# Quantised rows turned by transposing transfers instead of by TensorE, and the work between the attention loops dealt anew

## The reference, cut to what matters

```python
def block(x, ctx):
    x = x + attention(layernorm(x), ctx, ctx)        # 16 heads of 32, causal mask, Wq Wk Wv Wo with biases
    return x + ffn(layernorm(x))

def bit_linear(x, w):                                # act_quant: per row, 127 / max|x|, rounded; w: ternary
    return act_quant(x) @ weight_quant(w).T

def ffn(x):
    h = bit_linear(x, w1)                            # 512 -> 2048
    h = depthwise_conv1d(h, conv_w, conv_b)          # three taps along the rows
    return bit_linear(silu(h), w2)                   # 2048 -> 512
```

## Time and profile before

| what | value |
|---|---|
| time, median of 3 runs | 1520.56 us (1520.53 to 1521.53) |
| time of the profiled execution | 1520.43 us |
| its span, first to last instruction | 1518.6 us |
| mean granted clock of TensorE | 0.988 |
| PE busy | 1460.6 us, 96% of the span |
| DVE busy | 1278.0 us, 84% |
| ACT busy | 1185.3 us, 78% |
| POOL busy | 1028.7 us, 68% |

### The profile page before, as it was taken

How to read it: one execution, slowest core, us unless ns; L and a number is a source line. 1 busy time by engine, 2 the same in 40 slices (tenths; PEclk the granted TensorE clock), 3 DMA queues, 4 the chain that set the end, 5 groups by cost and what they waited for, 6 DMA issues and landing times. The chain is left out here.

```text
span 1518.6 us, 24856 instructions
## 1 busy us (share of the span) xinstructions
PE 1460.6 (96%) x9102; PEld 892.5 (59%) x9102; DVE 1278.0 (84%) x2002; ACT 1185.3 (78%) x2190; POOL 1028.7 (68%) x834
## 2 busy tenths in 40 slices
PE   9998988999999999999999999999999999999898
PEld 6474655657575665657575665657575655656343
DVE  5787796898979889898979898897979898887877
ACT  3567788979787888979687888979687888978763
POOL 4011567868675977968675977968675877968543
PEclk8999899999999999999999999999999999999999
DMA  8561002021310303030310303030210202020001
GB/s 258 148 193 42 29 8 71 8 80 32 76 43 12 94 8 99 8 93 19 75 44 18 88 8 99 8 100 14 73 43 23 84 8 71 8 71 1 31 1 56
DMA packets 80343, 85.21 MB, mean 56 GB/s; under 512 B 29983, under 2 KB 55839, under 8 KB 79709
## 3 DMA queue, kind: packets, MB, share of 16 engines
q1 hardware_dynamic: 80221, 83.62, 19.1%
HBM read 38.74 MB, written 19.42 MB: 38 GB/s over the span
## 5 line engine op out<-in xcount | busy, mean ns | idle before, releaser
L675 POOL TENSOR_TENSOR h<-h,gall 128x512 f32<-128x512 f32 x233 | 343.9, 1476 | 18.3
L660 POOL TENSOR_TENSOR h<-h,r 128x512 f32<-128x512 f32 x240 | 307.0, 1322 | 52.5 <-ACT r L1222 50.6
L673 POOL TENSOR_TENSOR gall<-gall,cw 128x512 f32<-128x512 f32 x233 | 255.3, 1096 | 112.6 <-DVE h L1751 112.6
L1751 DVE SCALAR_TENSOR_TENSOR h<-gall,cw,h 128x512 f32<-128x512 f32 x249 | 253.2, 1020 | 47.6 <-ACT h L1320 47.4
L885 PEld LDWEIGHTS ps<-va,pexp 128*128 128x128 f32 x2048 | 259.5, 192 | 29.0 <-issue 10.9
L1676 DVE SCALAR_TENSOR_TENSOR gall<-ps,bias,srow 128x512 f32<-128x512 f32 x256 | 191.1, 747 | 94.3 <-POOL h L675 57.9
L891 PE MATMUL ps<-xqT,w1T 128*128 128x512 f16 x1024 | 255.1, 379 | 6.6 <-DVE gall L1676 6.5
L885 PE MATMUL ps<-va,pexp 128*128 128x33 f32 x2048 | 257.7, 270 | 0.0
L1085 PE MATMUL ps<-w2T,hqb 128*128 128x512 fp8e4 x960 | 242.4, 380 | 0.0
L1320 ACT ACTIVATE h<-gall,cb,cw 128x512 f32<-128x512 f32 x249 | 216.3, 869 | 8.3
L1301 ACT ACTIVATE pexp<-ps 128x512 f32<-128x512 f32 x320 | 179.8, 589 | 54.5 <-PE ps L854 27.9
(11 more groups left out here) (226 smaller groups left out, 2336.8 us busy)
## 6 DMA issues: line engine op xcount, KB each, us to landing
qs<-hl SPq DMA_DIRECT2D x192, 128.0 KB, 2.4
xr<-in_x SPq DMA_DIRECT2D x16, 1024.0 KB, 5.4
out<-xr SPq DMA_DIRECT2D x64, 256.0 KB
h<-in_L_ffn_w SPq DMA_DIRECT2D x8, 1024.0 KB, 5.4
srow<-in_L_xattn_bo SPq DMA_DIRECT2D x15, 256.0 KB, 3.3
kst<-kh_scratch SPq DMA_DIRECT2D x32, 38.5 KB
xr<-in_ctx SPq DMA_DIRECT2D x1, 1024.0 KB
h<-in_L_xattn_Wk SPq DMA_DIRECT2D x1, 1024.0 KB, 8.2
```

Of the source, the lines that this page charges most:

```text
L660: gp.tensor_tensor(hc(c), hc(c), r2[:], ALU.mult).then_inc(u_ok, 1)
L673: gp.tensor_tensor(right, right, cw[:, c, 2:3].to_broadcast([P, TB]), ALU.mult).then_inc(c2m_ok, 1)
L675: gp.tensor_tensor(hc(c), hc(c), right, ALU.add).then_inc(c2p_ok, 1)
L1751: ve.scalar_tensor_tensor(out=hc(c), in0=g[:, c % 4, 1:TB + 1], scalar=cw[:, c, 1:2], in1=hc(c), op0=ALU.mult, op1=ALU.add).then_inc(c1_ok, 1)
```

## The change

1. turn_xq, its 16 transposes and its four PSUM copies are gone. As each of the four quantised row tiles is ready, SP issues a transposing transfer from it (hlq, now with adjacent elements) straight into xqT. mm1_ahead(0) waits for these.
2. The hidden absmax has three pieces: column tiles 0 to 3 in the attention loop ahead of the last tap, 4 to 11 after at_low, 12 to 15 after residual(0); two merges in place of one.
3. q_low moves ahead: two of them after residual(1), two after residual(2). Nothing lies between norm2 and quantise any more.
4. ACT squares tiles 0 and 1 before it centres tiles 2 and 3.
5. In the late_results slots PE runs mm2(0), the first two query_scores, spread_scales, half of mm2(1), and then steps n = 2 to 15: four matmuls of mm2 in each of n = 2 to 7, two in each from n = 8 on. result(1) comes after the fourth maximum.

```diff
         def hlq(i):
-            return osb[:, i, :].bitcast(F16)[:, 0:2 * D:2]
+            return osb[:, i, :].bitcast(F16)[:, 0:D]
@@ SP
+                if do_a:
+                    for i in range(TT):
+                        sp.wait_ge(xq_ok, at(s, TT, i + 1))
+                        sp.dma_start(xqT[:, :, i * P:(i + 1) * P], hlq(i), transpose=True).then_inc(xq_turned, 16)
                 if do_m and do_a:
                     store_rows(range(2 if late_results(s) else TT))
@@ PE
-                        pe.wait_ge(xqc, at(s, KT, KT))
+                        pe.wait_ge(xq_turned, at(s, 16 * TT, 16 * TT))
...
                 def turn_pm():
-                    pe.wait_ge(pm_ok, at(s, 3, 2 if s == NB else 0))
+                    pe.wait_ge(pm_ok, at(s, 5, 0))
...
+                elif late_results(s):
+                    mm2(0)
+                    query_scores(0, 0)
+                    query_scores(0, 1)
                 elif do_a and do_m:
                     mm2(0)
                     mm2(1)
...
-                if do_a and do_m and s != NB - 1:
-                    mm2(2, range(0, 8))
+                if late_results(s):
+                    mm2(1, range(0, 8))
                 if s == NB - 1:
                     mm2(2)
                     mm2(3, range(0, 11))
-                    turn_xq(range(KT))
...
                 for n in range(0 if s == NB - 1 else TT * NG):
-                    if do_q:
+                    if do_q and not (late_results(s) and n < 2):
                         query_scores(n // NG, n % NG)
...
-                    if do_a and do_m:
-                        if n < 4:
-                            mm2(2, range(8 + 2 * n, 10 + 2 * n))
-                        elif n < 13:
-                            mm2(3, MM2_LAST[n - 4])
+                    if late_results(s):
+                        if n in (2, 3):
+                            mm2(1, range(4 * n, 4 * n + 4))
+                        elif 4 <= n < 8:
+                            mm2(2, range(4 * n - 16, 4 * n - 12))
+                        elif 8 <= n < 15:
+                            mm2(3, range(2 * n - 16, 2 * n - 14))
+                        elif n == 15:
+                            mm2(3, range(14, 15))
+                            mm2(3, range(15, 16))
...
-                    if do_a and n in (13, 14):
-                        turn_xq((n - 13,))
-                    if do_a and n == 15:
-                        turn_xq((2, 3))
@@ ACT
                     centre(1)
...
+                    square(0)
+                    square(1)
+                    if late_results(s):
+                        offset(1)
                     centre(2)
...
                     centre(3)
-                    if late_results(s):
-                        offset(1)
-                    for i in range(TT):
-                        square(i)
+                    square(2)
+                    square(3)
...
-                    if do_a:
-                        act.wait_ge(xqt_ok, at(s, KT, k + 2 - k % 2))
-                        copy(xqT[:, k, :], xq_half(s, k)).then_inc(xqc, 1)
@@ DVE
+                def absmax(a, b, o):
                     dve.wait_ge(si_ok, at(s, CT, 2 * b - CT))
+                    if a == 6 and do_a:
+                        dve.wait_ge(pm_ok, at(s, 5, 3 - 5))
                     ve.tensor_reduce(o[:], h[:, a:b].rearrange("p a t e -> p t a e"), AX.XY, ALU.max,
                                      apply_absolute_value=True).then_inc(pm_ok, 1)
...
+                    if do_f and do_a and c == CT + 1:
+                        absmax(0, 2, pm)
                     if do_f and c >= 2 and not on_pe(s, c - 2):
                         taps(c - 2)
...
                 if do_f and do_a:
-                    absmax(0)
-                    if s == NB - 1:
-                        residual(0)
-                    absmax(1)
-                    if s == NB - 1:
-                        residual(1)
-                    merge()
+                    absmax(2, 6, r2)
+                    merge(r2, 2)
+                    residual(0)
+                    absmax(6, 8, r2)
+                    merge(r2, 4)
+                    residual(1)
...
-                    if s < NB - 1:
+                    if s == 0:
                         residual(0)
                         residual(1)
+                    if s > 0 and do_q:
+                        q_low(0)
+                        q_low(1)
+                    centred_max(0)
                     residual(2)
-                    centred_max(0)
+                    if s > 0 and do_q:
+                        q_low(2)
+                        q_low(3)
+                    centred_max(1)
                     residual(3)
-                    centred_max(1)
...
-                if s > 0 and do_q:
-                    q_low(0)
-                    q_low(1)
...
                 if do_a:
                     norm2()
-                if s > 0 and do_q:
-                    q_low(2)
-                    q_low(3)
...
                     result(0)
-                    result(1)
+                    if not late_results(s):
+                        result(1)
...
                     if do_q:
                         maximum(n // NG, n % NG)
+                    if late_results(s) and n == 3:
+                        result(1)
```

More of the change, by code:

```diff
@@ L321, in build @@
         dgs_ok = sem("dgs_ok")
-        xqt_ok = sem("xqt_ok")
-        xqc = sem("xqc")
+        xq_turned = sem("xq_turned")
         sr_ok = sem("sr_ok")
@@ L419, in score_tiles @@
             return range(NS * c // n, NS * (c + 1) // n) if c < n else range(0)
-        MM2_LAST = [range(2 * n, 2 * n + 2) for n in range(7)] + [range(14, 15), range(15, 16)]
         LATE = (TT - 1) * P
@@ L582, in slot @@
                         sp.wait_ge(q, 16 * NB)
-                    sp.wait_ge(xqt_ok, KT * NB)
+                    sp.wait_ge(xq_turned, 16 * TT * NB)
                     for bb in range(NBATCH):
@@ L922, in mm1_ahead @@
                         pe.wait_ge(src, at(s, 1, 1))
+                    if c == 1 and do_q:
+                        pe.wait_ge(mtc, at(s, 2, 3))
                     mm1(c)
@@ L1033, in turn_maxima @@
                     r.then_inc(mt_ok, 1)
-                def turn_xq(ks):
-                    for k in ks:
-                        if k == 0:
-                            pe.wait_ge(xq_ok, at(s, TT, TT))
-                        if k == 2 and do_q:
-                            pe.wait_ge(mtc, at(s, 2, 3))
-                        bank = xq_half(s, k)
-                        for i in range(TT):
-                            r = tp(bank[:, i * P:(i + 1) * P], hlq(i)[:, k * P:(k + 1) * P], identh[:])
-                        r.then_inc(xqt_ok, 1)
                 def spread_row():
@@ L1756, in taps, with merge @@
                                                 in1=hc(c), op0=ALU.mult, op1=ALU.add).then_inc(c2_ok, 1)
-                def absmax(k):
-                    dve.wait_ge(si_ok, at(s, CT, 8 * (k + 1) - CT))
-                    ve.tensor_reduce((pm, r2)[k][:], h[:, 4 * k:4 * k + 4].rearrange("p a t e -> p t a e"), AX.XY, ALU.max,
-                                     apply_absolute_value=True).then_inc(pm_ok, 1)
-                def merge():
-                    dve.wait_ge(pm_ok, at(s, 3, 2 - 3))
-                    ve.tensor_tensor(pm[:], pm[:], r2[:], ALU.max).then_inc(pm_ok, 1)
-                def absmax_last(a, b, o):
+                def absmax(a, b, o):
                     dve.wait_ge(si_ok, at(s, CT, 2 * b - CT))
+                    if a == 6 and do_a:
+                        dve.wait_ge(pm_ok, at(s, 5, 3 - 5))
                     ve.tensor_reduce(o[:], h[:, a:b].rearrange("p a t e -> p t a e"), AX.XY, ALU.max,
                                      apply_absolute_value=True).then_inc(pm_ok, 1)
-                def merge_last(o, n):
-                    dve.wait_ge(pm_ok, at(s, 3, n - 3))
+                def merge(o, n):
+                    dve.wait_ge(pm_ok, at(s, 5, n - 5))
                     ve.tensor_tensor(pm[:], pm[:], o[:], ALU.max).then_inc(pm_ok, 1)
@@ L1806, in attention @@
                     elif k == 0:
-                        dve.wait_ge(xqt_ok, at(s, KT, 0))
+                        dve.wait_ge(xq_turned, at(s, 16 * TT, 0))
                     dve.wait_ge(rz_ok, at(s, NG, k + 1))
@@ L1909, in slot @@
                     if s == NB and c == 16:
-                        absmax_last(0, 4, pm)
+                        absmax(0, 4, pm)
                         fix_absmax()
@@ L1935, in slot @@
                 if s == NB:
-                    absmax_last(4, 6, r2)
-                    merge_last(r2, 2)
+                    absmax(4, 6, r2)
+                    merge(r2, 2)
                     fix_scales()
-                    absmax_last(6, 8, pexp[:, 0, :])
-                    merge_last(pexp[:, 0, :], 4)
+                    absmax(6, 8, pexp[:, 0, :])
```

(1 more changed line is left out.)

3 lines of the change are left out of this document (removed).

## The result

The changed kernel takes 1556.38 us (median of 4 runs, 1554.38 to 1559.19) against 1520.55 us (4 runs) of the kernel before: a ratio of 1.0245, 95% interval 1.0226 to 1.0263. The profiled execution has a span of 1554.9 us and a mean granted clock of 0.978 (before 1518.6 and 0.988). It is slower, by the amount and for the reason forecast; three terms of the sum were off by 1 to 3 us each, partly against each other. One of all the runs reported here was a slow one (1539.56 us, of e6_both_even), and its ratio leaves it out.

A forecast was written before the change was run, and what follows sets the result against it. The prediction took PE and DVE, side by side between the loops, as the bound, with PE stalling on DVE. 1520.4 + 24.7 (slots) + 8.5 (clock) + 1.3 (edges) = 1555 us; 8-in-10 range 1521 to 1582.

The forecast's parts named there:

- DVE's chain: DVE's steps from the tap to the maxima in slot 6: first maximum at 663.2 against 663.79, 0.6 us sooner.
- The slots: PE stalls 1.2 us at turn_pm and 2.4 at the third query: +1.9 us per slot, 24.7 in 13.
- The clock: Granted clock halves behind the new PE stall in five of 13 slots, 1.7 us each: +8.5 us, bounds 0 and 22.
- The edges: Slot 0 about -1, slot 1 +1, slot 15 +2, masked slots 3, 7, 11 together -0.7: sum +1.3 us.
- the transfers' term of 0: Transposing transfers land before mm1_ahead(0) needs them, so cost 0; they would count from 3.4 us each in series.
- The total: Whole kernel: 1555 us, 2.3% slower; 8-in-10 range 1521 to 1582, the forecast's own range 1536 to 1578.
- the third rival: Transfers are late: at 5 us each in series, 6.2 behind the need in 15 slots, +93, about 1650 us; chance 0.12.
- the sum of 21 us: Estimate by the skill's table for transposing 16 blocks by DMA in series: 21 us, 7 us too late in every slot.
- negmT in the queue: In SP's queue the maxima stand behind the transfers and two result rows, but are ready at 677 only.
- the first: Rival: PE isn't held and the transposes are simply gone, stretch 20.55 in place of 22.10, 1500 us; chance 0.07.
- The second: Rival: DVE sets the end as before, PE's stalls stay inside its slack, 1522 us, up to 1535; chance 0.11.

The follow-up runs named there:

- e6_both_even: The changed kernel with residual(2) and two q_low right behind residual(1), two q_low behind norm2, first queries later and mm2 spread evenly: 1521.49 us, ratio 1.0002.
- e5: e1_cover with residual(2) moved ahead of the four q_low and centred_max(0): 1535.63 us, ratio 1.0105.
- e4: The changed kernel with q_low(0) and (1) behind residual(2), q_low(2) and (3) between norm2 and quantise: 1534.64 us, ratio 1.0106.
- e1_cover: The changed kernel with all 16 matmuls of mm2(1) ahead of the third query, the rest one step sooner: 1534.97 us, ratio 1.0116.
- e2: The kernel before with only the transposing transfers in place of the 16 transposes and four copies: 1527.60 us, ratio 1.0048.
- e9: e6_both_even with the result-row stores behind negmT in SP's queue and x_low(2) and (3) ahead of taps(11): 1515.21 us, ratio 0.9962.
- e3: The changed kernel with PE's order of mm2 and query_scores and the place of result(1) as before: 1548.47 us, ratio 1.0198.
- e10: e2 with the stores of result rows behind negmT in SP's queue, against the kernel before: 1524.30 us, ratio 1.0034.

## Why the prediction was right, and which terms were off

**DVE's chain, step by step, held.** Counted from spread_row (591.10 before, 603.19 after): at_low 48.86 predicted, 49.00 measured; residual(2) done 63.3, 63.42; turn_pm 63.5, 63.57; first maximum 72.1, 72.00; third query 72.95, 72.84; norm2's idle time 1.2, 1.13. In a slot at full clock spread_row comes at 86.32 against 86.25. e5 and e4 show that the slot hangs on this chain: reordered at equal length it gives the same 85.8, and shortened by 1.2 us it lets the first maximum begin 1.2 sooner and the slot end 1.0 sooner (85.32 against 86.32 at full clock). That DVE gains 0.6 us at the first maximum was right too (72.00 against 72.69). The 1.9 us per slot come from PE: it is late at the third query, and its steps of four matmuls behind it (1.13 us) are longer than a maximum (0.71).

**The slots** are 1.96 us longer at full clock, against 1.9. All 13 take 37.36 us more, of which 7 x 1.69 = 11.83 is the clock; 25.5 is left (predicted 24.7, and -0.7 for the masked ones). The stalls lie partly elsewhere, however. turn_pm waits 0.30, not 1.2, since PE itself comes 0.99 later: project_q waited 0.87 for x_low. The prediction took the loop as unchanged. This error had no price, as turn_pm had to wait for DVE anyway: in e1_cover the loop is 39.81 again and the wait 1.85. In slots 4, 8 and 12, where the loop is 41.7 in both kernels, the wait of after is 1.5.

**The clock** was mis-sized in its count: seven of 13 slots (2, 4, 6, 8, 10, 12, 13), not five, so 11.8 us in place of 8.5; each cost 1.69 us (24.45 against 22.76), as taken. All seven are among the ten slots where the third query waits 2.05 us; in the masked slots 3, 7 and 11 it waits 1.53, and the clock stays. That the fall hangs on this stall is shown by e1_cover, where with a wait of 0.33 it never came in slots 3 to 14, though PE waits 1.69 at turn_pm there. Why seven of the ten, and not each, stays open.

**The edges** were predicted at +2.0 without the masked slots, and are -1.1 (1554.9 - 1518.6 = 36.3, less 37.4). The step that failed is slot 15. at_low does come later there, but by 1.35 (2.2 said), and turn_pm to spread_row fell from 13.17 to 10.59: before, PE had waited 1.39 us there for the quantised rows and turned them for 0.90, both ahead of spread_row. So slot 15 is 1.54 shorter where +2 was said. That is no saving yet, for the transfers' term of 0 fails in the same place: right behind spread_row mm1_ahead(0) waits 2.87 us for them and runs at half clock (3.53 us for eight matmuls, before 1.89), and its next eight begin 0.65 later than before, counted from the start of slot 15. The rest of the kernel is 1.6 shorter; before, the clock had fallen there once more (at 1487.5). Slots 0 and 1 gave -1.9 and +1.8 (-1 and +1 said).

**The total** of 1555 against 1556.7 profiled is closer than its terms: the clock's +3.3 and the edges' -3.1 happened to cancel. Of its range, the upper end isn't what the terms give: 1520.4 + 24.7 + 22 + 1.3 is 1568, not 1578.

**The transfers** cost nothing in the changed kernel's late slots, as taken: 1.26 us each in SP's queue, 2.4 to land, where 3.4 had been worked out as the price at which they would count. Issued every 1.3 us and landing 2.4 later, they overlap in flight, so the series that the third rival rests on doesn't exist. The Trainium skill ("VectorE: DVE Perf Modes", The three transpose paths) puts a 128x128 transpose of bf16 by DMA at 1309 ns; here one instruction turns four blocks of that size (float16) and lands in 2.4 us, and four of them, issued 1.3 us apart, are all landed about 6.3 us after the first issue. So the sum of 21 us, block after block, doesn't hold here. What the prediction didn't see is where they do cost, besides slot 15: in the kernel before they add 0.48% [0.31, 0.65], through negmT behind them in SP's queue and through the clock. It named negmT in the queue and found it safe, which is so in the changed kernel only because q_low is sooner there (12 transfers begin 23.2 us ahead of spread_row, in e2 15.2).

Of the rivals, the first failed where the prediction said: the first maximum begins at 72.0, and would have had to begin before 70.3. The second needed a third-query stall below 0.5 us; e1_cover has it, and isn't at 1522 but at 1535, since that rival left out turn_pm's stall and PE's slower steps: behind the first maximum the slot takes 13.25 us, before 11.67.

## What to carry to other kernels

Where two engines run side by side and hand over at several places, follow the longer chain to its end, and take the engine that waits as a sum of waits: one wait removed comes back at the next hand-over (1.85 us at turn_pm became 1.03 + 0.90), until the chain itself gets shorter. An instruction moved out of a gap leaves the gap: the two q_low that had filled POOL's 1.0 us cost 1.2 us on the bound engine when they went to an earlier place. When a transfer is added to a queue, list what is issued behind it and when that is needed; here the stores ahead of negmT were the ones that could wait (medians 3 to 4 us lower without them, though with intervals that overlap).

## What was not expected of the hardware

- DVE's instructions that read two SBUF tiles stretch beside POOL's. The tap takes 0.74 us alone; with one of POOL's adds starting beside it, it took 1.83, and the merge 0.69 alone and 1.50 in e1_cover and e6. DVE, then POOL, in slot 6 of the changed kernel:

```profile
637.77 0.80 DVE L1741 SCALAR_TENSOR_TENSOR h<-gall,cw,h 128x512 f32<-128x512 f32 x1
...
640.83 1.83 DVE L1741 SCALAR_TENSOR_TENSOR h<-gall,cw,h 128x512 f32<-128x512 f32 x1
642.58 1.27 DVE L1776 TENSOR_TENSOR hl<-ps,hl 128x512 f16<-128x512 f32 x2
```

```profile
638.10 1.63 POOL L672 TENSOR_TENSOR h<-h,gall 128x512 f32<-128x512 f32 x1
639.69 1.04 POOL L670 TENSOR_TENSOR gall<-gall,cw 128x512 f32<-128x512 f32 x1
640.80 1.30 POOL L672 TENSOR_TENSOR h<-h,gall 128x512 f32<-128x512 f32 x1
```

  The one at 640.83 starts 0.03 us behind POOL's add (640.80 to 642.10) and ends 0.56 behind its end; then x_low (L1776) ends late, and project_q waits. So the loop of equal work is 39.8 or 40.8 us long, by how the two engines' instructions happen to fall. This holds in slots 2 to 14 of all kernels but e9, 143 in all: the wait for x_low is 0.83 to 0.92 us where this tap takes 1.78 us or more (53 slots), 0.28 to 0.36 where it takes 1.24 to 1.28 (33), and at most 0.14 where it takes 0.74 to 0.85 (57). x_low itself, which reads PSUM, and absmax, which reads one tile, kept their times. The Trainium skill ("GPSIMD Engine Reference", 1. Specifications) says that POOL's SBUF interfaces are shared with VectorE's, with contention for instructions that have two SBUF inputs; the rows agree.
- The granted clock falls from 1.00 to 0.50 (2.4 to 1.2 GHz) for 3.4 us behind a wait of PE of 2.05 us in seven of ten slots, and in e4 behind three of four waits of 2.0 to 2.35. It did not fall behind waits of 1.03 to 1.89 us (the other slots of e4; turn_pm in e1; the masked slots of after), though in slot 15 of before it did behind one of 1.66, and not behind 1.03 and 0.90 with 4.6 us of work between (e5, none of 13). Behind the 0.97 at the last maximum it fell three times of 13 in e2, three in e3 and once in e10, but in e1 never behind 1.04 in the same place. The length of the last wait alone doesn't tell it.
